# A decoder layer of attention, retention and FFN on one core: constants loaded in parts, late x tiles from ScalarE's queue, FFN rows turned by DMA

## The reference, cut to what matters

```
x = layernorm(x + attention(x))            # 16 heads, causal, gated by a policy of mean(x)
x = layernorm(x + retention(x, ctx, ctx))  # 16 heads of 32, cross attention
x = layernorm(x + ffn(x))                  # 512 -> 1408 -> 512, fake quantized

retention:  q, k, v = query@W_Q, key@W_K, value@W_V          (per head)
            q, k = xpos(q), xpos(k)         # x * cos_s + rot(x) * sin_s
            sim = (q @ k^T) * decay         # gammas[h] ** (n - s), causal
            ret = groupnorm(sim @ v)
            out = (ret * silu(query @ g_w.T + g_b)) @ out_w.T + out_b
ffn:        xq = fake_quant(x)              # one scale for the whole of x
            h  = fake_quant(silu(xq @ Wg^T) * (xq @ Wu^T))
            out = h @ Wd^T                  # Wg, Wu, Wd quantized by row
```

## Time and profile before

| | |
|---|---|
| median of 3 runs (lowest, highest) | 1779.34 us (1777.58, 1780.52) |
| the profiled execution's own time | 1775.6 us |
| its span (outside the span: 1.8) | 1773.8 us |
| mean granted clock of TensorE | 0.985 |
| attention, retention | 0 to 957.3, 957.3 to 1510.5 us |
| FFN: gate and up, down | 1510.5 to 1677.3, 1677.3 to 1773.8 us |
| PE busy | 1639.9 us (92%) |
| DVE, POOL, ACT busy | 1321.0 (74%), 1079.0 (61%), 1054.4 us (59%) |
| DMA | 192.05 MB, mean 108 GB/s |

### The profile page before, as it was taken

The page is one execution under the profiler, slowest core; times in us unless marked ns, Lnnn a source line. Parts: engine busy times, 40 slices in busy tenths (PEclk is TensorE's granted clock), DMA queues, the critical chain, the costliest instruction groups (busy, mean ns, idle before and its releaser), DMA issues. The chain is left out here.

```text
span 1773.8 us, 36662 instructions
## 1 busy us (share of the span) xinstructions
PE 1639.9 (92%) x13158; PEld 729.5 (41%) x13158; DVE 1321.0 (74%) x2954; ACT 1054.4 (59%) x1861; POOL 1079.0 (61%) x1020
## 2 busy tenths in 40 slices
PE   5999999989999999999897889999999996899997
PEld 2433344433434334343233444454454543444443
DVE  6778656777567775777835688888787776788798
ACT  6576555566555665567563366566465564555587
POOL 4078777678776778768804776886877784000044
PEclk9999999999999999999999999999999999999999
DMA  8412112221122210222235555567465441651275
GB/s 290 122 27 60 52 27 61 69 85 51 25 60 71 83 53 24 61 71 60 86 110 169 112 126 164 130 160 169 126 153 130 110 123 52 254 202 48 72 280 201
DMA packets 204383, 192.05 MB, mean 108 GB/s; under 512 B 103721, under 2 KB 154409, under 8 KB 203305
## 3 DMA queue, kind: packets, MB, share of 16 engines
q1 hardware_dynamic: 198536, 180.97, 35.5%
q10 hardware_dynamic: 5664, 8.73, 1.6%
HBM read 106.12 MB, written 38.14 MB: 81 GB/s over the span
## 5 line engine op out<-in xcount | busy, mean ns | idle before, releaser
L1183 DVE CUSTOM_DVE_ANT_0 a_mx<-a_mx,a_mqk 128x128 f32<-128x128 f32 (+3 forms) x512 | 241.8, 511 | 136.8 <-PE a_mx L1392 133.2
L998 ACT ACTIVATE a_P<-a_mx 128x512 f32<-128x512 f32 (+3 forms) x418 | 185.6, 494 | 132.5 <-PE a_mx L1410 77.1
L1406 PE MATMUL a_mx<-a_Qs,a_Ks 128*128 128x512 f16 (+3 forms) x768 | 226.5, 331 | 18.1 <-ACT a_P L998 7.8
L1392 PE MATMUL a_mx<-a_Ks,a_Qs 96*128 96x512 f16 (+3 forms) x768 | 222.4, 329 | 5.9 <-DVE a_nm L1183 2.3
L1266 POOL TENSOR_TENSOR a_P<-a_P 128x512 f32<-128x512 f32 (+3 forms) x164 | 157.6, 988 | 89.8 <-PE a_o L1422 77.3
L998 ACT ACTIVATE share<-a_mx 128x512 f32<-128x512 f32 (+3 forms) x302 | 135.3, 495 | 99.2 <-PE a_mx L1410 56.3
L1266 POOL TENSOR_TENSOR a_P<-a_P,share 128x512 f32<-128x512 f32 (+3 forms) x192 | 178.9, 961 | 23.3 <-ACT share L998 18.3
L1186 DVE TENSOR_REDUCE a_nm<-a_mx 128x1 f32<-128x512 f32 x256 | 164.7, 681 | 31.9 <-PE a_mx L1392 31.0
L2352 PE MATMUL r_pj<-r_xT,share 128*128 128x512 f16 x768 | 184.4, 379 | 3.4 <-DVE r_AD L2216 1.8
L2352 PE MATMUL r_pj<-share,cth 128*128 128x512 f16 x672 | 164.2, 385 | 10.3 <-DVE r_AD L2216 4.7
L3098 PE MATMUL f_pj<-f_xqT,f_wgu 128*128 128x512 bf16 x704 | 156.7, 379 | 0.6 <-DVE f_xqT L2982 0.6
(11 more groups left out here) (305 smaller groups left out, 3856.7 us busy)
## 6 DMA issues: line engine op xcount, KB each, us to landing
x_scratch<-rows SPq DMA_DIRECT2D x60, 256.0 KB, 2.9
rows<-x_scratch SPq DMA_DIRECT2D x56, 256.0 KB, 3.5
lead<-in_xT SPq DMA_DIRECT2D x24, 512.0 KB, 4.6
lead<-in_ctxT SPq DMA_DIRECT2D x38, 256.0 KB, 2.9
h_scratch<-f_h SPq DMA_DIRECT2D x3, 2816.0 KB, 9.1
f_h<-h_scratch SPq DMA_DIRECT2D x3, 2816.0 KB, 10.6
a_Ks<-a_kph SPq DMA_DIRECT2D x256, 32.0 KB, 1.9
a_Qs<-a_qph SPq DMA_DIRECT2D x256, 32.0 KB, 1.9
```

Of the source, the lines that this page charges most:

```text
L998: act.activation(Pf[pf.at[key]][:, off:512], pb[:, off:512], ACT.Exp).then_inc(p_exp, 1)
L1183: dve.tensor_tensor_reduce(bank_of(it)[:, 0:n], bank_of(it)[:, 0:n], mqk[:, 512 - n:512], 1.0, -3e38, ALU.add, ALU.max, nm[:, col:col + 1] ...
L1392: pe.matmul(pb[:, 0:n], Qs[s][0:96, j, qt * P:(qt + 1) * P], Ks[s][0:96, j, hf * 512:hf * 512 + n], start=True, stop=True).then_inc(max_mm, 1)
L1406: m = pe.matmul(pb[:, off:512], Ks[s][:, j, kt * P:(kt + 1) * P], Qs[s][:, j, qb * 512 + off:(qb + 1) * 512], start=True, stop=not diag)
```

## The change

1. Attention: tiles k = 2 and 3 of x of the batches 1 to 3 (six loads) are issued by ACT at a place in its list, with the wait for the staging buffer there (`stage_free`: DVE's part of the tile two before).
2. Retention: the issue of the constants waits for nothing now and holds the first halves of cosQ and sinQ, gb and qd (770 KB instead of 2562); Dm comes in four parts of 256 KB at places 1.2 ahead of their groups, and the second halves of cosQ and sinQ with ob (768 KB) at place 0.6. Each part has its semaphore, and the readers wait for theirs. The planner takes a DMA transpose on SP as 1.25 + 2.2 instead of 2.4 + 2.6, and ACT's `xnorm` is called up by place.
3. FFN: the 28 tiles of blocks 1 to 7 are transposed by a DMA from `f_xq` straight to `f_xqT`, issued by SP; 112 PE transposes and ACT's 28 copies go. SP waits for the cast and for the buffer of `f_xqT` before each issue. A buffer of `f_xq` is free when the transfer has landed instead of when PE has read it.

```diff
@@ -458,7 +458,7 @@
             done.add(("splitx", b, k))
             if k == 3:
                 done.add(("splitx", b))
-        W.append((place, lambda: put("SP", ("loadx", b, k), 0.48, lambda: after(3.4, landed), lambda: room(stage),
+        W.append((place, lambda: put("ACT" if k > 1 else "SP", ("loadx", b, k), 0.53, lambda: after(3.9, landed), lambda: room(stage),
                                      lambda: stage.take(key))))
 
     def loadm(b, k, place):
...
@@ -1013,6 +1013,12 @@
                 else:
                     w.wait_ge(w_lo, SPLITW[("w1", 1)])
                 act.activation(Oh[:, g, qb * 512:(qb + 1) * 512], onb[on.at[key]][:, :], ACT.Copy).then_inc(o_hi, 1)
+            elif kind == "loadx":
+                b, k = key
+                i, prior = stage.at[("x", b, k)], stage.before[("x", b, k)]
+                if prior:
+                    w.wait_ge(*stage_free(prior))
+                act.dma_start(stageb[i][:, :], A["xT"][b, k * P:(k + 1) * P, :]).then_inc(x_in[i], 16)
             elif kind == "wonorm":
                 w.wait_ge(eps_pool, 1)
                 for k in range(4):
...
@@ -1561,7 +1567,7 @@
-            put("SP", ("kt", b, t), 2.4, lambda: after(2.6, kt_in), lambda: half_done(b - 1, t // 4))
+            put("SP", ("kt", b, t), 1.25, lambda: after(2.2, kt_in), lambda: half_done(b - 1, t // 4))
...
@@ -1608,7 +1614,7 @@
-            put("SP", ("xt", *key), 2.4, lambda: after(2.6, lambda: done.add(("xT", *key))),
+            put("SP", ("xt", *key), 1.25, lambda: after(2.2, lambda: done.add(("xT", *key))),
...
@@ -1781,19 +1787,22 @@
     def last_rows():
         def made(k):
             done.add(("xstats", k))
-            if has(*(("xstats", i) for i in range(4))):
-                put("ACT", ("xnorm",), 1.6, lambda: put("DVE", ("xnorm",), 0.3, scale))
 
         def scale():
             for k in range(4):
                 put("ACT", ("xn", k), 0.75, lambda k=k: put("SP", ("xn", k), 0.5))
         for k in range(4):
             put("DVE", ("xstats", k), 0.9, lambda k=k: made(k))
-
-    loads.sort(key=lambda v: v[0])
+        loads.append((-8, lambda: put("ACT", ("xnorm",), 1.6, lambda: put("DVE", ("xnorm",), 0.3, scale),
+                                       lambda: has(*(("xstats", i) for i in range(4))))))
+
     flow.order["SP"] += [("ctx", 0, 2), ("ctx", 0, 3), ("consts",)]
     put("ACT", ("constk",), 0.6)
     last_rows()
+    for g in range(4):
+        loads.append((g - 1.2, lambda g=g: put("SP", ("decay", g), 0.5)))
+    loads.append((0.6, lambda: put("SP", ("rest",), 1.4)))
+    loads.sort(key=lambda v: v[0])
 
     def first(t):
         put("ACT", ("split", 0, t), 0.55, lambda: put("DVE", ("split", 0, t), 0.62, lambda: (done.add(("split", 0, t)), ctx(t + 2))))
...
@@ -1896,7 +1906,7 @@
-    NCONSTK, NCONST = 16, 16 * 6
+    NCONSTK, NCONST, NREST = 16, 16 * 4, 16 * 3
...
@@ -1965,13 +1975,16 @@
                 w.wait_ge(xn_act, num[it])
                 sp.dma_start(x1d[r0:r0 + P, :], xlast[k][:, :]).then_inc(xlast_out[k], 16)
             elif kind == "consts":
-                w.wait_ge(constk_in, NCONSTK)
-                for i in range(2):
-                    w.wait_ge(ct_in[i], 16)
-                for dst, src in ((cosQ[:, :], A["c_cosQ"]), (sinQ[:, :], A["c_sinQ"]), (gb[:, :], A["gb"]),
-                                 (qd[:, :], A["c_qd"]), (Dm[:, :, :], A["c_D"]),
+                for dst, src in ((cosQ[:, 0:512], A["c_cosQ"][:, 0:512]), (sinQ[:, 0:512], A["c_sinQ"][:, 0:512]),
+                                 (gb[:, :], A["gb"]), (qd[:, :], A["c_qd"])):
+                    sp.dma_start(dst, src).then_inc(const_in, 16)
+            elif kind == "decay":
+                hs = slice(4 * key[0], 4 * key[0] + 4)
+                sp.dma_start(Dm[:, hs, :], A["c_D"][:, hs, :]).then_inc(decay_in[key[0]], 16)
+            elif kind == "rest":
+                for dst, src in ((cosQ[:, 512:L], A["c_cosQ"][:, 512:L]), (sinQ[:, 512:L], A["c_sinQ"][:, 512:L]),
                                  (ob[:, :], A["ob"].partition_broadcast(P))):
-                    sp.dma_start(dst, src).then_inc(const_in, 16)
+                    sp.dma_start(dst, src).then_inc(rest_in, 16)
             elif kind == "xT":
                 b, hf, k = key
                 r0, n = b * L + hf * 512 + k * P, num[it]
...
@@ -2202,7 +2215,7 @@
-                w.wait_ge(const_in, NCONST)
+                w.wait_ge(*((rest_in, NREST) if hf else (const_in, NCONST)))
...
@@ -2210,7 +2223,7 @@
-                w.wait_ge(const_in, NCONST)
+                w.wait_ge(decay_in[g], 16)
...
@@ -2338,7 +2351,7 @@
-                w.wait_ge(const_in, NCONST)
+                w.wait_ge(rest_in, NREST)
...
@@ -2502,14 +2515,24 @@
 
         def made():
             xq.give(src)
-            copier[src] = "copy.a" if src[1] and lighter() else "copy.d"
-            put("ACT" if copier[src] == "copy.a" else "DVE", (copier[src], src), 0.5 if copier[src] == "copy.a" else 0.36, copied,
-                lambda: has("sdrmm") if src[1] == 1 else src[1] < 2 or has(("upmm", src[1] - 2, IT - 1)))
+            put("DVE", ("copy.d", src), 0.36, copied)
 
         def copied():
             tr.give(src)
             done.add(("copy", src))
-        N.append((place - 0.12, lambda: integers(src, 512, ready, lambda: done.add(("whole", src)))))
+
+        def landed():
+            xq.give(src)
+            done.add(("copy", src))
+
+        def whole():
+            done.add(("whole", src))
+            if src[1]:
+                put("SP", ("turnd", src), 1.25, lambda: after(1.8, landed),
+                    lambda: has("sdrmm") if src[1] == 1 else has(("upmm", src[1] - 2, IT - 1)))
+        N.append((place - 0.12, lambda: integers(src, 512, ready, whole)))
+        if src[1]:
+            return
         pe_item(T, place, ("turn", src), 0.24, made, lambda: room(tr) and has(("whole", src)), lambda: tr.take(src))
 
     def lighter():
...
@@ -2813,16 +2837,21 @@
             if src[1] >= 2:
                 w.wait_ge(d_mm, num[("down", src[1] - 2, 3)])
         elif xq.before[src]:
-            w.wait_ge(turn_mm, num[("turn", xq.before[src])])
+            w.wait_ge(*turned(xq.before[src]))
 
     def target(src):
 
         return xqT[src[1] % 2][:, :, src[2] * P:(src[2] + 1) * P]
 
+    def turned(src):
+
+        if src[1]:
+            return turn_in[4 * (src[1] % 2) + src[2]], 16 * ((src[1] + 1) // 2)
+        return turn_mm, num[("turn", src)]
+
     def copied(src):
 
-        kind = copier[src]
-        return (copy_act if kind == "copy.a" else copy_dve), num[(kind, src)]
+        return turned(src) if src[1] else (copy_dve, num[("copy.d", src)])
 
     def after(key):
 
...
@@ -2874,6 +2903,11 @@
             elif kind == "d":
                 c = key[0]
                 sp.dma_start(wd[:, c, :, :], wq["d"][c]).then_inc(d_in[c], 16)
+            elif kind == "turnd":
+                src = key[0]
+                w.wait_ge(*made_whole(src))
+                copy_free(w, src)
+                sp.dma_start_transpose(target(src), xqb[xq.at[src]][:, :]).then_inc(turn_in[4 * (src[1] % 2) + src[2]], 16)
             elif kind == "spill":
                 blk = key[0]
                 w.wait_ge(h_dve, num[("gated", blk, IT - 1)])
...
@@ -2920,11 +2954,6 @@
-            elif kind == "copy.a":
-                src = key[0]
-                w.wait_ge(turn_mm, num[("turn", src)])
-                copy_free(w, src)
-                act.activation(target(src), turned_bank(src), ACT.Copy).then_inc(copy_act, 1)
```

17 lines of the change are left out of this document (9 added, 8 removed).

## The result

| | before | with the change |
|---|---|---|
| median of 6 runs (lowest, highest) | 1780.51 us (1777.58, 1787.32) | 1769.90 us (1767.52, 1773.32) |
| profiled execution, span | 1773.8 us | 1766.5 us |
| mean granted clock of the profiled execution | 0.985 | 0.977 |

The ratio is 0.9938, with a 95% interval of 0.9919 to 0.9956: 11 us faster, where 20.9 were forecast. The time lies just above the range that was given. A second set of runs on another chip gave 0.9930 (0.9910 to 0.9950).

A forecast was written before the change was run, and what follows sets the result against it. The prediction took PE to bound all phases, so gains were PE work removed or PE idle closed: -5.0 - 7.0 - 2.5 - 6.4 = -20.9, from 1779.34 to 1758.4 us, range 1748 to 1769.

The forecast's parts named there:

- attention: Attention's batches 1 to 3: earlier loads of x tiles 2 and 3 close PE idle time, -5.0 us.
- retention, start: Retention's start: x rows land earlier, PE's gap before their first transposes closes, -7.0 us (ends 4.0 and 9.0).
- retention, the rest: Retention's last half: one of PE's two waits for AD goes, -2.5 us (ends 0 and -5.4).
- FFN, gate and up: FFN's gate and up: PE drops transposes of 28 tiles at 0.23 us each, -6.4 us (ends -7 and -4).
- next to nothing: Attention's batches 2 and 3: almost no gain counted after ACT's new wait; batch 1's idle and clock (5.2) counted nearly whole.
- The gap of 7.05 closes: Retention's start: PE's 7.05 us wait for x rows goes and ctx tile, K tile, Q and A move with it.
- Rival (b): Retention's start: POOL binds, so only 3 of the 7 us stay, total 1762.4; chance 0.14.
- The first AD wait: Retention's last half: PE's 2.99 us wait for AD goes, as 48 out products stand between A and R.
- the reordering: Middle of retention: new order from the planner's cheaper transposes, taken as nothing, 3 us either way in the bounds.
- the list of what is late next: Retention: Dm's parts and the constants' second halves were checked as possible late arrivals and taken as covered by PE time.
- The upper ends: Whole kernel: largest gains of the terms, 8.2, 9, 5.4 and 7, less a microsecond, given as -28.4 us.
- Rival (d): FFN's block starts: turned tiles land late and hold the first gate product; slower, above 1783; chance 0.05.

The follow-up runs named there:

- e8: e5 with K tiles 2 and 3 put ahead of S tiles 1 and 2 in DVE's list at retention's start; 0.9906 of the kernel before.
- e2: The kernel before with the retention part of the change alone (constants in parts, planner's times); 0.9989 of the kernel before.
- e3: The kernel before with the FFN part of the change alone (28 tiles turned by DMA); 0.9971 of the kernel before.
- e6: e4 with retention's first two loads of x rows issued ahead of all constants; 0.9911 of the kernel before.
- e5: e4 with four ACT scalings and four DVE maxima spread over pauses of the last two groups of retention's last half; 0.9897 of the kernel before.
- e4: The changed kernel with the second halves of cosQ and sinQ and ob issued behind w_up's first tile on SP; 0.9934 of the kernel before.
- e1: The kernel before with the attention part of the change alone (x tiles 2 and 3 issued by ACT); 0.9996 of the kernel before.
- e10: e8 with attention as before (all x tiles loaded by SP); 0.9922 of the kernel before.
- e7: e4 with attention as before (all x tiles loaded by SP); 0.9922 of the kernel before.

## Why the prediction was wrong: step by step

The sum was -20.9, and about -11 to -12.5 came. Averages over the profiles of the table, with and without a part, are steadier than the one pair of profiles, since one and the same code varies by 3 to 5 us in attention (957.4 to 960.3 in five profiles, 953.2 to 957.9 in eight):

| term | forecast | shown | from |
|---|---|---|---|
| attention | -5.0 | -3.6 | 958.9 (5 profiles, tiles by SP) to 955.3 (8, tiles by ACT) |
| retention, start | -7.0 | -4.1 | A at 47.8 (3) to 43.7 (8, without e8's edit) |
| retention, the rest | -2.5 | +0.7 | A to the end 506.3 (3) to 506.9 (the change twice, e2) |
| FFN, gate and up | -6.4 | -5.9 | 167.8 (3) to 161.9 (11) |
| FFN, down | 0 | +0.9 | 96.7 (3) to 97.6 (11) |
| sum | -20.9 | -12.0 | |

- **Attention: the mechanism was right, the size near.** In batch 1 the loads at ACT's place came ten us earlier, and the idle second parts filled. The last `a_mx<-share` product (L1294 of the kernel before) of batch 0, ahead of which no list changes, ends anywhere from 161.6 to 166.8 us. Measured from there to the end of attention, the five profiles with tiles by SP take 794.8 to 797.6 us and the eight with tiles by ACT 791.1 to 793.4: -4.4 on average instead of the table's -3.6. From that product of one batch to that of the next, batch 1 fell from 220.5 to 217.7, and batches 2 and 3 together by 1.1. Forecast was "next to nothing" for them, so the term was mis-sized by batch 1, which gave 2.8 of the 5.2 that were counted there. In time only 1 to 3 us of it arrive, with intervals that reach to nothing and a clock lower by 0.002 in the timed runs. The Trainium skill's page "DMA: Bandwidth & Descriptors", section "Issuing engines are not separate DMA queues", says that starting DMAs from several engines saves only the sequencer's time for the issue, usually small beside the transfer. By that the part would be worth next to nothing; the profiles go against it at this place, where loads stood behind waiting issues, and the times lie between the two.
- **Retention's start: this step failed.** "The gap of 7.05 closes, and the rest of the chain (...) moves with it": the gap closed, the chain didn't move with it, and a wait of 3.13 us for POOL came in its place. Rival (b) was right, with a gain of 4 instead of 3: the K tiles' chain over DVE and POOL was hidden behind the transfers by only about 4 us. At the same length of low clock ahead of A it is 3.9 (46.7 to 42.8, with 6.8 us of it) and 3.3 (47.3 to 44.0, with about 10); e3's 49.4 has 13.6 us of it and raises the mean in the table. e6 showed that the transfers have left the path, e8 that the order on DVE is a small part of the chain. The step that I left out is to follow the second longest path: DVE's K tiles (L2168) started 5.4 us apart, at 985.65 and 991.04, already in the kernel before, the second behind the wait of 2.85 for POOL in the earlier trace rows.
- **Retention's rest: this step failed twice, with a right core.** The first AD wait went, but the last 408 matmuls, which hold it, became only 0.8 us shorter (53.9 to 53.1) instead of 2.5: the reordering, taken as nothing, put ACT's four scalings (2.92 us) ahead of the root of group 2, on the path to the last z, and 2.1 us of the gain went there (51.0 in e5). And the list of what is late next named Dm's parts and the second halves themselves, not what is queued behind them: w_up's first tile, for which DVE waits in order, 2.7 us (e2, e4).
- **Slips in the working.** The AD waits are those of groups 2 and 3, not 0 and 1; nothing in the sum hangs on the name. The upper ends add up to -28.6, not -28.4. And the forecast's base was the median of three runs, 1779.34, where six runs gave 1780.51; 0.9938 of the former would be 1768.3.
- **FFN: right.** 28 tiles at 0.23 us make 6.4; at the same stretch of lower clock the phase is 6.1 to 6.3 us shorter (see e3), and the table's -5.9 compares unequal clocks. The transposes landed 2.5 us after the issue, below the 2.8 taken, and no block waited. Rival (d) did not come near.
- **FFN's second half: not forecast, and a matter of the clock.** It is 96.2 to 96.4 us in two profiles of kernels with the old FFN (before, e2), 97.6 in the third (e1), and 97.5 to 97.7 in all the others. The code of that half is the same. The two short ones have 3.4 us at the lower clock among its first down products and 3.4 more some 19 us in; all the others have 6.8 us in one piece at the first products. These 36 products take 9.51 us in the kernel before (9.29 in e2) and 10.75 in e1 (10.6 to 10.8 in the change and e10), first before, then e1:

```profile
1680.13 9.51 PE L3117 MATMUL f_pj<-f_wd,f_hq 128*128 128x512 bf16 x36 [1.72 <-DVE f_hq L2977]
```

```profile
1677.71 10.75 PE L3123 MATMUL f_pj<-f_wd,f_hq 128*128 128x512 bf16 x36 [1.73 <-DVE f_hq L2983]
```

Why the stretch falls one way or the other no run tells; e1 has the longer one with the old FFN, so it isn't the FFN part alone.

- **The base.** The profiled execution of the kernel before had a clock of 0.985; 50 timed runs of it had 0.975 to 0.985. It was at the upper edge, with 53 us at the lower clock where the other profiles have 62 to 89. Comparing any other profile with it shows the other's clock as a loss.

The range missed by one us: the low ends of the start (-4.0) and of the rest (0) were taken as unlikely to come together, and both came, with +0.9 in FFN's second half that no term had.

## What to carry to other kernels

When a wait is removed at the start of a phase, follow the next path to the same instruction and price the gain as the distance between the two, not as the wait. When a queue's order changes, list what stands behind each moved item, on that queue and on the engines that wait in order, whatever it is for; and when a planner's number moves the order, look at the last few groups of the phase on every engine, since nothing hides them. Before a profile is compared, compare its clock with that of several runs, and compare stretches that hold the same work, in several profiles: the phases of one profile are off by 2 us and more.

## What was not expected of the hardware

- The times of one kernel follow the mean granted clock, with a wide scatter: over 28 runs of the kernel before on one chip, 0.7 us more for each 0.001 less, with a correlation of 0.55. PE idle time that the change closed did not raise the clock; the mean over the timed runs was 0.9765 and 0.9777 in the two sets of the change, against 0.9798, 0.9788 and 0.9805 in three sets of the kernel before.
- In this kernel a stretch at 1.2 GHz cost less than the matmuls in it. Batch 2 of attention, in the same old code, took 220.5 and 221.3 us in the profiles without any (before, e7) and 221.9, 221.7 and 222.8 us with 6.8 us of it (e2, e3, e10): 1.2 more on average, while PE's busy time rose by 2.6; the rest came out of PE's waits. These are five profiles, and those of one kind lie up to 0.8 and 1.1 us apart.
- DMA transposes of 128 x 512 bf16 tiles beside FFN's traffic landed in 2.5 us (median of 28, the slowest 5.8), as fast as the 34 of the FFN weights in the same kernel (2.5).
